# Graph network kernel: the gather engine's wait for its rows stands in every second group alone

## The reference, cut to what matters

```
# message network (one pass over the edges)
message = relu(concat([x[row], x[col], edge_feat]) @ W_msg + b_msg), batch-normalised
agg     = segment_sum(message, col)
# attention network (three layers, one pass over the edges each)
e     = leaky_relu(alpha_s[src] + alpha_d[dst])
ex    = exp(e - segment_max(e, dst)[dst])
out   = segment_sum(h[src] * ex / segment_sum(ex, dst)[dst], dst) + b
x     = relu(out)
```

## Time and profile before

| | us |
|---|---|
| median of three runs | 11586.8 |
| profiled execution, its own time | 11603.76 |
| its span, first to last instruction | 11601.9 |
| POOL busy | 6445.6 (56%) |
| PE busy | 7023.9 (61%) |
| DVE busy | 4659.8 (40%) |
| ACT busy | 3723.7 (32%) |
| gathers (L720), busy | 4786.4 from `table_a`, 1607.0 from `table_m` |

### The profile page before, as it was taken

How to read it: one execution, slowest core, us unless ns; L and a number is a source line. 1 busy time by engine, 2 the same in 40 slices (tenths; PEclk the granted TensorE clock), 3 DMA queues, 4 the chain that set the end, 5 groups by cost and what they waited for, 6 DMA issues and landing times. The chain is left out here.

```text
span 11601.9 us, 140692 instructions
## 1 busy us (share of the span) xinstructions
PE 7023.9 (61%) x32264; PEld 6154.0 (53%) x32264; DVE 4659.8 (40%) x12446; ACT 3723.7 (32%) x7463; POOL 6445.6 (56%) x6482
## 2 busy tenths in 40 slices
PE   4888888888845555555564555555556555555555
PEld 2377777777644444444464444444445444444445
DVE  5744444444533333333333333333333333333334
ACT  2622222222123333333323333333332333333332
POOL 0266666666446666666636666666653666666662
PEclk8555555555556666665556666666665666666665
DMA  6111111111111111111111111111111111111111
GB/s 112 35 35 34 35 34 34 35 34 34 24 31 32 32 32 32 33 32 32 32 25 32 32 32 33 32 32 32 32 30 27 32 32 32 32 32 32 33 32 24
DMA packets 338292, 393.34 MB, mean 34 GB/s; under 512 B 225463, under 2 KB 232543, under 8 KB 336055
## 3 DMA queue, kind: packets, MB, share of 16 engines
q0 software_dynamic: 206976, 330.75, 14.1%
q1 hardware_dynamic: 131270, 62.12, 2.9%
HBM read 366.44 MB, written 25.99 MB: 34 GB/s over the span
## 5 line engine op out<-in xcount | busy, mean ns | idle before, releaser
L720 POOL DMA_INDIRECT rows<-table_a,idx x4851 | 4786.4, 987 | 3171.7 <-DMA rows<-table_a,idx 1490.5
L1257 PE MATMUL ps<-ident,work 128*128 128x128 f32 x4872 | 1215.4, 427 | 2966.0 <-ACT work L1213 2936.5
L1257 PEld LDWEIGHTS ps<-ident,work 128*128 128x128 f32 x4872 | 940.8, 222 | 3103.7 <-issue 2086.3
L720 POOL DMA_INDIRECT rows<-table_m,idx x1617 | 1607.0, 994 | 1497.7 <-issue 483.3
L1274 PE MATMUL ps<-rows,work 128*128 x9744 | 1866.8, 366 | 837.8 <-issue 593.1
L1274 PEld LDWEIGHTS ps<-rows,work 128*128 128x128 f32 x9744 | 1733.1, 274 | 1033.7 <-issue 1033.7
L1213 ACT ACTIVATE work<-work,small 128x896 f32<-128x896 f32 x696 | 725.0, 1042 | 4192.7 <-DVE big L1131 4143.4
L1150 DVE SCALAR_TENSOR_TENSOR work<-dstf,big,select 128x224 f32 x696 | 314.3, 452 | 3665.7 <-SPq L666 3656.8
L1265 PE MATMUL ps<-ident,work 128*128 128x128 f32 x4872 | 1175.4, 418 | 110.7 <-DVE work L1160 110.7
L1139 DVE CUSTOM_DVE_ANT_0 work<-work,ps 128x896 f32<-128x896 f32 x696 | 757.1, 1088 | 1207.3 <-issue 917.1
L1265 PEld LDWEIGHTS ps<-ident,work 128*128 128x128 f32 x4872 | 1047.3, 229 | 115.6 <-DVE work L1160 115.6
(11 more groups left out here) (245 smaller groups left out, 7165.0 us busy)
## 6 DMA issues: line engine op xcount, KB each, us to landing
rows<-table_a,idx POOLq DMA_INDIRECT x4851
rows<-table_m,idx POOLq DMA_INDIRECT x1617
edge_parts<-big SPq DMA_DIRECT2D x6, 1617.0 KB, 7.7
big<-edge_parts SPq DMA_DIRECT2D x231, 42.0 KB
work<-edge_parts SPq DMA_DIRECT2D x50, 192.0 KB
table_a<-work SPq DMA_DIRECT2D x3, 2474.5 KB, 22.3
b_dram<-big SPq DMA_DIRECT2D x3, 1176.0 KB, 8.0
big<-b_dram SPq DMA_DIRECT2D x3, 1176.0 KB, 18.5
```

The lines of the kernel that those rows point to most:

```text
L720: pool.indirect_dma_start(rows[:, k % RING, j, 0:width], None, table, bass.IndirectOffsetOnAxis(ap=idx[:, k // CHUNK, at:at + 1], axis=0)) ...
L1257: last = pe.transpose(ps[:, 4 + j // 4, (j % 4) * P:(j % 4 + 1) * P], prob[:, par, j, :], ident[:])
```

## The change

`settle` is called only behind groups with an odd number in the body of 16, so POOL waits for landings after every second group. `hand_over` of SP is as before.

```diff
@@ def gather(g, k, c):
                         for j in range(TPG):
                             at = k % CHUNK * TPG + j
                             pool.indirect_dma_start(...).then_inc(s_gat[k % RING], 16)
-                        settle(k % RING, 2 * c + k // RING, TPG)
+                        if k % 2 == 1:
+                            settle(k % RING, 2 * c + k // RING, TPG)
```

## The result

The changed kernel takes 10573.09 us (10571.16 to 10575.14, four runs), beside 11583.09 us (11576.21 to 11587.46, four runs) for the kernel before: the ratio is 0.9129, with a 95% interval from 0.9113 to 0.9144, and 1010 us are gone. The forecast was 10622 us. The profiled execution took 10571.16 us with a span of 10569.1 us, 1033 us less than the span before.

The account below looks back on a forecast made before the run. POOL's gathers were taken to bound the kernel. Attention 742 us plus message pass 223 us made 965 us, off a median of 11586.8 us: 10622 us, range 10543 to 10884 us.

Parts of the forecast that it names:

- The bound: All passes: every engine waits for rows, paced by POOL's gathers; group to group 11.19 us.
- A removed gap, 2.15 us: POOL, between two groups: the gap falls from 2.45 us to 0.30 us once the wait is gone.
- The lower bound: POOL, what is left of a removed gap: 0.30 us, as between any two gathers of a group.
- The rival with 0.87 us: POOL's sequencer is not ahead across groups, so a gap closes only to 0.87 us: 10884 us; chance 0.08.
- 460 gaps: POOL: waits removed behind even groups, 115 in a pass and 460 in four passes, giving 989 us.
- Transfers, nothing: DMA: about two gathers under way at any time as before, busy share 0.16 to 0.18; no cost.
- Attention, 742 us: Three attention passes: POOL stays the bound, so all 345 gaps count, 742 us saved.
- no change: Gathers lengthened beside DVE's work: their total stays as it is, with 139 us either way as a bound.
- Message pass, 247 - 24 = 223 us: Message pass: 247 us from gaps, less 0.1 us a group (24 us) because PE's own work is tight.
- The loop's jump: POOL, jump back every 16 groups: a gap of 2.88 us and further idle time, behind odd groups, which stay.
- The slower rival: Denser gathers meet DVE, lengthening one pair in every group by 1.34 us: 249 us slower, 11836 us; chance 0.03.
- What would show it: Timeline signs: fourteen gathers 0.30 us apart, some 460 waits, a pass of 2370 us, gather mean 0.98 to 1.0.

Follow-up runs that it names:

- none: Changed kernel with settle never called, so POOL never waits for a landing: 11575.03 us (0.9989 of the kernel before), later 9463.54 us (0.8172).
- even: Changed kernel with the wait behind even groups instead of odd ones: 11255.91 us (0.9711 of the kernel before), later 10474.6 us (0.9041).

## Why the prediction was right, point by point

- **The bound.** POOL's rhythm sets the time, before and after: the saving is the change in the gathers' first-to-last time to within 4 us.
- **A removed gap, 2.15 us.** Right: it went from 2.49 and 2.46 us to 0.305 us, 2.18 and 2.16 us each. The lower bound was the one to take; L709 at 5016.9, six us ahead of the engine, told it. The rival with 0.87 us is out: no such gap is found at a border.
- **460 gaps.** Right: 115 in each pass, 453 waits are left.
- **Transfers, nothing.** Right: the DMA engines' share went from 0.16 to 0.17 and 0.18, and the median gather stays at 945 ns.
- **Attention, 742 us.** Too low by 122 us: 3 x 288 = 864. Gaps give 753; the other 107 to 111 us are gathers no longer held by L1160, which stood in the sum as "no change".
- **Message pass, 247 - 24 = 223 us.** Too high by 58 us, and for a wrong reason. The deduction was for PE; PE follows at 9.8 us in `none`. The gaps gave 249 us, and longer gathers took 84 back. The step that failed is "I take no change" for the gathers; its bound of 139 us either way held in total, for +84 and -107 us nearly cancel (-23 us), and that is why the sum fell within 45 us of the difference of the medians (965 to 1010) and within 68 of that of the profiled executions. That the two cancel is luck; nothing in the sum foresaw it.
- **The loop's jump.** The prediction took the idle time after the jump for part of it. It belongs to every tenth group instead. Both stayed as they were in the changed kernel, so the sum is untouched.
- **The slower rival.** Its mechanism is real, at 1.046 us a gather in the message pass, and short of the mean of 1.14 from which it would decide. The long gathers were said to follow DVE's work; by which operation was to be had from the trace before: the earlier trace rows have 1.83 and 1.41 us, and DVE's rows beside them name L823 and L862.
- **What would show it.** Fourteen gathers, the seventh gap of 0.30, some 460 waits: as said. A pass of 2370 us: 2330 in attention, 2458 in the message pass. DVE's wait at L1151 fell by 1.2 us a step (3656.8 to 2813.7 over 693), at L831 only by 0.4 (513.6 to 431.6 over 231), not by 1.1; the pace of that pass fell by 0.7 us a group (11.37 to 10.65). The mean of a gather stayed at 0.985 us over all passes, and so within what was said.

## What to carry to other kernels

A wait on the engine that issues the bounding work costs its whole round trip each time, and if another engine waits for the same event anyway, it is not needed for the result: here the last such wait could go too, for 18% of the time, in the set without late signals. In the two sets with them the kernels without these waits lost most or all of the gain. When the pace of one engine moves against another's, look for pairs that lock each other, by kind of operation and by phase; "no change" for a duration holds only if the phase stays. And time a candidate in more than one session beside the kernel before: `none` came out at 0.9989 in one and at 0.8172 in another, on the same chip.

## What was not expected of the hardware

- A gather is held until 0.82 us after the end of a long operation of DVE with two inputs in SBUF (0.85 to 1.09 us) that is running 0.13 us after its start and has been for some 0.18 us; a reduction of 1.45 us with one input, or the same product with an input from PSUM, holds none. A `tensor_scalar` of 0.27 us with one input in SBUF holds too.
- POOL's sequencer runs ahead across a border of groups, a semaphore wait that is already met and the raising of `begun`, with no more than the 0.30 us between two gathers. The loop's jump is hidden as well (0.30 us in `even` and `none`), but not behind a wait (2.9 us in place of 2.5).
- Behind the first gather of every tenth group stands a gap of 1.0 to 1.4 us where that group follows a wait (1.25 us in the changed kernel at 5005.22), and 0.30 us where it does not (`even`, `none`). What the sequencer does there no row shows.
- Under conditions that the kernel does not set, signals of PE reach ACT 9 to 10 us late, and register operations of SP take up to 1.4 us in place of 0.03. The kernel before, with its wait behind each group, was 0.1% slower then (11592.57 and 11595.78 us beside 11583), kernels with fewer waits up to 2800 us slower than expected.
